# A residual added on TensorE, squares in a buffer of their own, and one branch per unit in place of one per pair of tiles

## What is computed

```python
x = x + _L0_conv_ref(_gn(x), w0, w1, w2, bias)      # wavelet convolution on three levels
x = x + _L1_conv_ref(_gn(x), spatial_weight)        # local similarity filter

# _L0: for each level: (ll, lh, hl, hh) = haar_dwt(curr); y = conv2d(stacked, w, 5x5); then the inverse transform
# _L1, over the 25 points around each point:
patches = _extract_patches(x)
dot = jnp.einsum('bchw,bckhw->bkhw', x, patches)
norm_x = jnp.sqrt(jnp.sum(x * x, axis=1))
norm_p = jnp.sqrt(jnp.sum(patches * patches, axis=1))
sim = dot / jnp.maximum(norm_x[:, None] * norm_p, 1e-8)
weight = (sim + 1.0) * 0.5 * spatial_weight[None, :, None, None]
out = jnp.einsum('bckhw,bkhw->bchw', patches, weight)
```

## Time and profile before

| | us |
|---|---|
| median of 3 runs (2222.95 to 2223.33) | 2223.08 |
| the profiled execution | 2207.9 |
| its span, first to last instruction | 2206.2 |
| TensorE busy in it | 1613.0 (73%) |
| VectorE busy | 1406.8 (64%) |
| ScalarE busy | 740.0 (34%) |
| POOL busy | 448.3 (20%) |
| iteration 4 (both layers), 1009 to 1258 us | 249 |

### The profile page before, as it was taken

The page is one execution under the profiler, slowest core; times in us unless marked ns, Lnnn a source line. Parts: engine busy times, 40 slices in busy tenths (PEclk is TensorE's granted clock), DMA queues, the critical chain, the costliest instruction groups (busy, mean ns, idle before and its releaser), DMA issues.

```text
span 2206.2 us, 49286 instructions
## 1 busy us (share of the span) xinstructions
PE 1613.0 (73%) x16895; PEld 853.4 (39%) x16895; DVE 1406.8 (64%) x2121; ACT 740.0 (34%) x1222; POOL 448.3 (20%) x792
## 2 busy tenths in 40 slices
PE   4776786778677786878668786878678786874465
PEld 3542343434333343434334343434334343432244
DVE  6427756866488456966478556966478445875354
ACT  2321243424243243423343243424243243423341
POOL 1343413012311213013311213012311113011000
PEclk8988997989888898979888897989888887987566
DMA  5243337673767547663766547673767448572665
GB/s 166 76 107 95 117 104 187 159 185 105 182 165 195 131 107 197 164 177 104 180 166 191 145 107 191 169 183 96 184 162 192 116 106 205 137 200 76 147 168 135
DMA packets 151105, 329.93 MB, mean 150 GB/s; under 512 B 47092, under 2 KB 96244, under 8 KB 150260
## 3 DMA queue, kind: packets, MB, share of 16 engines
q1 hardware_dynamic: 109296, 207.18, 36.9%
q0 software_dynamic: 41472, 118.24, 19.7%
HBM read 238.70 MB, written 86.61 MB: 147 GB/s over the span
## 4 chain that ended last, share of the span: by engine, by line
PE 29%; DMA 20%; SPq 19%; DVE 16%; issue 11%; ACT 3%; DVEq 1%; POOL 1%; ACTq 0%; POOLq 0%
DMA d_n<-st_n 11%; PE conv L1295 9%; DMA unit_mem<-d_n 8%; PE conv L1269 5%; SPq L410 5%; PE gram L1360 4%; SPq L384 4%; SPq L403 3%; PE out_ps L1382 3%; SPq L382 3%; PE conv L1254 2%; SPq L400 2%; PE stat_ps L1318 2%; DVE wgt L1017 2%; PE vals_ps L1343 2%
## 5 line engine op out<-in xcount | busy, mean ns | idle before, releaser
L1295 PE MATMUL conv<-thl,wconv 128*128 128x496 f16 (+2 forms) x1920 | 551.2, 417 | 23.9 <-DVE xa L896 12.5
L1017 DVE SCALAR_TENSOR_TENSOR wgt<-gram,tapw 124x512 f32<-124x512 f32 x512 | 350.0, 686 | 286.7 <-PE gram L1360 245.7
L468 POOL DMA_DIRECT2D ring<-in_x x576 | 333.7, 584 | 568.4 <-DVE bn L778 339.9
L1360 PE MATMUL gram<-unit_mem 128*60 128x128 f16 x4096 | 259.7, 253 | 221.9 <-DMA unit_mem<-d_n 128.2
L1360 PEld LDWEIGHTS gram<-unit_mem 128*60 128x60 f16 x4096 | 158.1, 117 | 444.8 <-issue 443.6
L1269 PE MATMUL conv<-thl,wconv 128*128 128x480 f16 (+7 forms) x1200 | 265.8, 377 | 0.0
L1295 PEld LDWEIGHTS conv<-thl,wconv 128*128 128x128 f16 x1920 | 169.4, 105 | 225.3 <-issue 73.2
L1318 PE MATMUL stat_ps<-st_n,sq_c 128*128 128x306 f32 x256 | 120.5, 560 | 170.0 <-ACT st_n L553 138.2
L1382 PE MATMUL out_ps<-wgt,vals 124*32 124x128 f32 x4096 | 194.6, 312 | 30.4 <-issue 24.4
L553 ACT ACTIVATE vals<-vals_ps 124x512 f32<-124x512 f32 x128 | 76.4, 597 | 363.3 <-PE vals_ps L1343 363.2
L1269 PEld LDWEIGHTS conv<-thl,wconv 128*128 128x128 f16 x1200 | 118.8, 101 | 132.0 <-issue 22.5
(11 more groups left out here) (133 smaller groups left out, 2057.8 us busy)
## 6 DMA issues: line engine op xcount, KB each, us to landing
unit_mem<-d_hl SPq DMA_DIRECT2D x128, 360.0 KB
unit_mem<-d_hl SPq DMA_DIRECT2D x256, 180.0 KB
ring<-in_x POOLq DMA_DIRECT2D x288, 128.0 KB, 3.3
ring<-in_x POOLq DMA_DIRECT2D x288, 127.0 KB, 3.6
d_hl<-st_hl SPq DMA_DIRECT2D x128, 180.0 KB
d_v<-st_v SPq DMA_DIRECT2D x128, 180.0 KB
unit_mem<-d_v SPq DMA_DIRECT2D x64, 360.0 KB
up<-d_z POOLq DMA_DIRECT2D x160, 128.0 KB, 3.2
```

The costliest lines, as they stand in the source:

```text
L468: pool.dma_start(dst, src).then_inc(raw_in[slot], 16)
L1017: V.scalar_tensor_tensor(out=dst, in0=g, scalar=SIM_SCALE ** 2, in1=tapw[:, :].unsqueeze(1).to_broadcast([KN, 2, 2 * QN]), op0=ALU.add, op ...
L1295: last = mm(dst[:, :, b0:b1], wconv0[:, w, 2 * (p % ROWS4) + s, dx + 2, :], thl[:, p % 2, d, s, :, b0 + dx:b1 + dx] if p % ROWS4 != 1 else ...
L1360: last = mm(bank[row:row + KQ, col:col + QN], key[:, q, e_at, TH * KW * g:TH * KW * g + KQ], tile[:, :, TH * g + 1:TH * g + 1 + TH, 1:1 + ...
```

## The change

Three edits, made together.

- **Residual on TensorE.** `save_x1`, `load_residual`, `residual_in` and the buffers `x1_res` and `d_x1` are gone. At k = 4 of each unit the new `residual(b, u)` writes zeros to the whole bank `out_ps` with one matmul of a row of zeros by 512 columns, and adds to it, straight from `x1`, sixteen fp32 matmuls 128x32 by 128 columns (4 column groups g, 4 quadrants q, q innermost) with the identity scaled once at the start. `filter_group` then only accumulates. `result` is now ScalarE's, ahead of `vals_out(b, j, 0)`, with the mean as bias. `finals`, which overwrites `x1`, waits for TensorE's reads (`res_read`).
- **Squares in `st_sq`.** `half_in` no longer waits for the save; `square_half` squares into the one buffer `st_sq`; the wait for the save stands in `norms`, before `st_n` is written. `st_v` is written there too, and `value_lows` goes from k = 0 to k = 6.
- **One branch per unit.** TensorE and VectorE write out each unit twice, guarded and not, and choose once at its start. `Chain.mark` and `back` let both sides count the same semaphore steps.

```diff
+            def square_half(b, h):
                 act.wait_ge(x2_done, 8 * b + h + 1)
-                copy(st_n[:, half, :], part, scale=1 / X_SCALE, func=ACT.Square).then_inc(sq_done, 1)
-                copy(in_strips(st_v[:, 0, half, :]), strips(part)).then_inc(v_high, 1)
+                if h > 0:
+                    act.wait_ge(n2_ready, 16 * b + 2 * h)
+                copy(st_sq[:, :], st_x2[:, h % 2, :, :].rearrange("p h w -> p (h w)"), scale=1 / X_SCALE, func=ACT.Square)\
+                    .then_inc(sq_done, 1)
...
                 if p == 0:
                     act.wait_ge(unit_vec, START + 8 * b + h)
+                    act.wait_ge(half_saved[h % 2], START + SAVES * (4 * b + h // 2))
...
+            def residual(b, u):
+                r, half = u // 2, u % 2
+                pe.wait_ge(unit_out, START + 8 * b + u)
+                pe.wait_ge(x1_done, 4 * b + 4)
...
+                mm(out_ps[:, :], zero_row[:, :], wconv0[0:1, 0, 0, :, :].rearrange("p t o -> p (t o)")[:, 0:BANK], start=True, stop=False)
+                o = out_ps[:, :].rearrange("p (q n) -> p q n", q=Q)
+                for g in range(BANDS):
+                    row = BH * r + TH * g
+                    for q in range(Q):
+                        last = mm(o[C * g:C * g + C, q, :].rearrange("p (h w) -> p h w", h=TH), ident[:, C * q:C * q + C],
+                                  x1[:, row:row + TH, UW * half:UW * (half + 1)], start=False, stop=False)
+                last.then_inc(res_read, 1)
...
+                for j in range(CONV_TILES):
+                    if ls:
+                        pe.wait_ge(flag_done, START + 8 * b + j + 1)
+                        alone(pe)
+                        short_ones = pe.value_load(flag[0:1, j % FLAGS:j % FLAGS + 1], min_val=0, max_val=P * UN)
+                        with pe.If(short_ones > 0):
+                            unit(j, True)
+                        with pe.Else():
+                            unit(j, False)
```

More of the change, by code:

```diff
@@ L780, in set_live @@
             def set_live(i):
+                if not first(i):
+                    dve.wait_ge(unit_out, START + 8 * (i - 1))
                 V.tensor_copy(mean_ls, mean_conv).then_inc(live_set, 1)
@@ L930, in finals @@
                     dve.wait_ge(x2_done, 8 * (n - 1) + 6 + 2 * half)
-                    for r in (2 * half, 2 * half + 1):
-                        dve.wait_ge(x1_saved[r], 16 * n)
+                    dve.wait_ge(res_read, 8 * (n - 1) + 4 + 4 * half)
                 s2 = sd[:, :, :, :].rearrange("p g s w -> p g (s w)")
@@ L999, in set_flag, with weights @@
                     .then_inc(flag_done, 1)
-            def weights(b, u, k, short_ones):
+            def weights(b, u, k, guarded):
                 n, e = 8 * (8 * b + u) + k, k // 2
@@ L1090, in iteration, with unit @@
                     raw_stats(i + 1, 3)
-                short_ones = None
-                for j in range(CONV_TILES):
+                def unit(j, guarded):
                     h = j + AHEAD
-                    if ls:
-                        dve.wait_ge(flag_done, START + 8 * b + j + 1)
-                        alone(dve)
-                        short_ones = dve.value_load(flag[0:1, j % FLAGS:j % FLAGS + 1], min_val=0, max_val=P * UN)
                     for k in range(PAIRS):
@@ L1149, in iteration @@
                         tap_weights()
-                if ls:
-                    result(b, CONV_TILES - 1)
+                for j in range(CONV_TILES):
+                    if ls:
+                        dve.wait_ge(flag_done, START + 8 * b + j + 1)
+                        alone(dve)
+                        short_ones = dve.value_load(flag[0:1, j % FLAGS:j % FLAGS + 1], min_val=0, max_val=P * UN)
+                        chains = gn1_chain, gn2_chain, prep_chain, wino_chain
+                        marks = [chain.mark() for chain in chains]
+                        with dve.If(short_ones > 0):
+                            unit(j, True)
+                        for chain, mark in zip(chains, marks):
+                            chain.back(mark)
+                        with dve.Else():
+                            unit(j, False)
+                    else:
+                        unit(j, False)
             def peak(n):
@@ L1362, in products @@
                     return last
-                with pe.If(short_ones > 0):
+                if guarded:
                     pe.wait_ge(wgt_done, START + n)
@@ L1434, in iteration, with unit, hook @@
                         hook_1(n)
-                for j in range(CONV_TILES):
-                    def hook(n, j=j):
+                def unit(j, guarded):
+                    def hook(n):
                         if n not in HOOKS:
```

113 lines of the change are left out of this document (49 added, 64 removed).

## The result

| | before | changed |
|---|---|---|
| median, us | 2223.01 | 2326.97 |
| lowest to highest of 4 runs | 2211.45 to 2223.33 | 2322.52 to 2342.04 |
| profiled execution, span | 2206.2 | 2320.9 |
| TensorE busy | 1613.0 | 1794.6 |

The changed kernel is slower: 1.050 times the time before, 95% interval 1.045 to 1.055 (the two medians alone give 1.047). The sign was forecast, the size was not: 27 us more were forecast, 104 were measured.

A forecast was written before the change was run, and what follows sets the result against it. Neither TensorE (73% busy) nor VectorE (64%) was taken to bound it throughout; -12 + 10.5 + 22 - 5 - 12 = +3.5 us per iteration, +28 over eight, 2236 on the profiled span, 2251 as median, said as 2250; range 2170 to 2345.

The forecast's parts named there:

- The residual's price: Residual matmuls on TensorE: 0.9 us, 1.15 with the zeros, 1.3 with the clock per unit; 10.5 us per iteration.
- the other end: Residual matmuls if each waited for the one ahead on its group and held the rest: 3.3 us per unit.
- Rival 2: Residual on TensorE runs one by one: +20 us per iteration, 2410 us in all; chance 0.12.
- The jump's price: Far jump over a guarded unit on TensorE: 2.8 us per unit, between 2.3 and 3.6; 22 us per iteration.
- Rival 1: Far jump on TensorE is cheap: 8 x 0.5 instead of 22 us per iteration, 2163 us in all; chance 0.12.
- The waits that the jumps swallow: TensorE's waits for unit data: of 16 us per iteration some 12 are swallowed by the added work.
- rival 3: VectorE pays for its jumps too, at another moment: +9 to +10 us per iteration, 2330 us in all; chance 0.17.
- some 2.5 us: TensorE in a unit: loss from the half clock that follows a gap of 3 us.
- The squares: Squares in their own buffer, with the earlier save: 12 us per iteration off, between 6 and 16.
- The sum: All terms per iteration: -12 + 10.5 + 22 - 5 - 12 = +3.5 us; eight iterations +28.
- The marks: Signs in the page after: issue idle 150 to 200 us, residual within 1 us, iterations 250 to 255, last unit 19.

The follow-up runs named there:

- e1: Changed kernel with the residual's loops swapped, so that four matmuls in a row go to four column groups: 2242.40 us, 1.0145 of the kernel before.
- e8: Changed kernel with each unit written once, unguarded, the flag still read but no branch following: 2192.52 us, 0.9900 of the kernel before.
- e4: Changed kernel with the unguarded unit first, so the jump stands at its end, on TensorE and VectorE: 2316.22 us, 1.0480 of the kernel before.
- e12: Changed kernel with twenty tiny matmuls more in TensorE's setup, shifting the code: 2365.23 us, 1.0667 of the kernel before.
- e10: Kernel before with only the one-branch-per-unit edit: 2307.23 us, 1.0402 of the kernel before.
- e2: Changed kernel with eight short branches per unit again on TensorE and VectorE: 2245.07 us, 1.0129 of the kernel before.
- e5: Kernel before with only the squares edit, residual and branches as before: 2209.54 us, 0.9965 of the kernel before.
- e3: Changed kernel with both column groups inside in the residual and eight short branches per unit: 2203.86 us, 0.9949 of the kernel before.

## Why the prediction was wrong

**The residual's price (the step that failed first).** I took 0.9 us from a row in which four column groups take turns, and argued that "a matmul waiting for its group does not hold back those for another". The code has q inside, four matmuls in a row on one group, and the argument holds for about half of a group's passes: 2.57 us at full clock, against 1.15 taken and 3.55 at the other end (3.3 and the zeroing). e1, which has the order of my row, costs 1.76 - 0.57 = 1.19. So the row was read rightly, and applied to another sequence. Eight units: 20.6 instead of 10.5 us per iteration. Rival 2 ("runs one by one") had the mechanism, not its extent: the groups did overlap, and the filter's matmuls even began ahead of residual passes that stand before them. The end at which each pass holds back all behind it would have missed by 1.0 us (3.55 - 2.57) and my reading missed by 1.4 (2.57 - 1.15); the starts in the rows contradict both.

**The jump's price (the second).** I took the loop's 3.57 us and subtracted for a covering queue, to 2.8. No queue shortens it: five of the eight starts in iteration 4 wait 3.7 to 4.3 us, more than the loop's 3.57. The register's read explains at most 0.4 of that (e8; none at e4's unit 0). The other three wait 5.3, 6.2 and 6.9; the 6.2 of unit 5 fell to 3.9 when the code was shifted (e12), for the other two the cause stays open. On average it is 4.8 us (276.5 / 58). As a net change of `issue` waits ahead of `gram` and `filter_group`: (276.5 + 0.4 - 31.1 - 24.4) / 8 = 27.7 us per iteration, against 22 - 5 = 17. Rival 1 (cheap) fell, and its price was on the wrong side: the dear side had no rival.

**The waits that the jumps swallow.** For unit data I said 12 us per iteration; (128.2 - 31.4) / 8 = 12.1. That this fits is in part luck: I had reckoned that 1.3 and 2.8 us per unit would swallow them, and it took 2.6 and 4.8. Not in the sum were the waits for weights, which fell as well, (60.9 - 12.0) / 8 = 6.1, and those for a flag ahead of `norm_piece`, 19.5 / 8 = 2.4: with TensorE late at each unit, VectorE is ahead everywhere. For the same reason rival 3 fell: VectorE's jump is not waited for.

**The clock.** The granted clock is the share of full speed that the profile records for TensorE. At 0.50 four convolution matmuls took 1.88 us, at 1.00 they took 1.02 to 1.04 (before the change, at 1196.07 in unit 5 and from 1243.79 on in unit 7). What my reading calls 1.2 GHz is a granted clock of 0.50: matmuls of 512 columns began 0.43 us apart there (1196.47, 1196.90), 1.2 columns per ns, and 0.22 apart at 1.00 (1244.02, 1244.23), 2.4 per ns. The average explains nothing: 0.850 before and 0.854 after. But two effects cancel in it. The branch edit alone lowers it, to 0.820 to 0.829 in e10, where the kernel before had 0.839 to 0.853; the other two edits without it (e2) have 0.868 to 0.886. The last unit of iteration 4 shows how. Before, it followed a gap of 0.48 us and ran at 1.00 throughout, 14.6 us. After the gap of 3.79 us TensorE's granted clock is 0.50 until 1300 and 0.62 until 1305, and the unit takes 21.0 us: 2.6 more for the residual and 3.9 for the lower clock. Four convolution matmuls of it, early and late (timeline of TensorE, the changed kernel):

```profile
1295.16 1.88 PE L1291 MATMUL conv<-thl,wconv 128*128 128x512 f16 x4
1299.51 1.86 PE L1291 MATMUL conv<-thl,wconv 128*128 128x496 f16 x4
...
1310.93 1.02 PE L1291 MATMUL conv<-thl,wconv 128*128 128x496 f16 x4
```

I had this loss ("some 2.5 us") in the working of what hides the jump, but not in the sum. That the sum below comes out without it says that the other units give about as much back; which ones was not looked at.

**The squares.** -12 forecast, (138.2 - 33.6) / 8 = 13.1 measured, and below the 50 us that I had set as a mark. In this kernel the reading is right; as a gain of the edit it is not, since alone it brings 6 us in all (e5). Here the late save was hidden behind the jumps: TensorE's waits for `norms`' copy into `st_n` are 0.6 us in the changed kernel, and 30.1 in e2 and 42.8 in e3, which have short branches.

**The sum** with the measured terms: -13.1 + 20.6 + 27.7 - 12.1 - 6.1 - 2.4 = +14.6 us per iteration. From the first convolution matmuls of one iteration to those of the next, over five iterations, it was (1848.2 - 526.0) / 5 = 264.4 us, against (1756.7 - 510.4) / 5 = 249.2 before: +15.2. Of the 11 us that were missing in my +3.5, the residual has 10 and the jumps 11; 8.5 of waits that I had not counted went the other way. Iteration 8 lost some 11 us: from the last matmuls of iteration 7 to the end it was 200.1 us before (from 2006.1) and 211.4 after (from 2109.5).

**The marks.** Idle for `issue` at nearly every start: right, though 276 us and not 150 to 200. Sixteen residual matmuls within 1 us: wrong. Squares below 50 and unit data below 60: right. Iterations of 250 to 255 us: wrong, 264. Last unit 19 us: wrong, 21.0 from its first `gram` (1294.59 to 1315.61, where the 3.19 us of the loop's own jump begin), and 24.8 with the jump ahead of it, which my 19 included (14.5 + 1.3 + 2.8). And I took 4.4 us for what a measurement can tell from no change, from three runs that lay close together; 19 runs of the kernel before (e1's job) spread over 24 us, 2202.64 to 2226.42.

## What to carry to other kernels

A price read from a row holds for the row's sequence: compare which part of the engine each instruction in a row goes to, not only shape and count, and let small matmuls on separate column groups take turns (1.76 us against 3.14 in e1). An `If` whose skipped side is short was cheap on TensorE here (e2 against e8: 23 us of `issue` for 512 of them); one that skips some 800 instructions (an estimate) cost it 3.7 to 6.9 us each time in iteration 4, and the matmuls ahead of it did not cover that (3.87 to 6.02 in e4), so write out two sides only on an engine that waits anyway, as VectorE did here (541.1 us for `gram`). After each such gap look at the granted clock too (0.50 behind the 3.79 us of the last unit), and price it unit by unit, since an average over the span can hide it (0.850 and 0.854). A wait that goes from one instruction should be followed to the next user of the same buffer before it is booked as a gain (in e5 138.2 us became 33.7 and 54.8).

## What the runs showed of the hardware that I had not expected

- Passes of fp32 matmuls of 128 columns on one column group followed each other at 0.11 us; another group's, next in the program, began 0.47 us after it, at about half of eight such passes (changed kernel, unit 1, worked out from the starts). With the groups taking turns 32 passes started in 0.9 us (e1), grouped in 2.2.
- Matmuls began out of the order of the program: in the changed kernel a filter matmul at 1160.89 ahead of residual passes at 1160.99, 1161.10 and later.
- A jump over some 800 TensorE instructions (my estimate from the matmuls of a guarded unit) left it idle for 3.7 to 6.9 us in iteration 4, more than the loop's jump over the whole body (3.1 to 3.6), which has no register read ahead of it; against the kernel with no jump each brought two more fetches of 16.4 KB (294 packets against 166, e8).
- Some 80 instructions more ahead of a loop, with no work in them to speak of, made this kernel 1.6% slower (2365.23 us against 2326.97, e12).
- Sixteen short branches per unit, eight on each of two engines, with the guards' code between them, cost 53 us in all (2245.07 - 2192.52, e2 and e8; 0.8 us per unit), though the earlier trace rows shows nothing.
- In the last unit of iteration 4 a gap of 3.79 us was followed by some 10 us at a granted clock of 0.50 and 0.62, and by 3.9 us more for the same work.
